# Row maxima of two neighbouring heads computed as a pair of short products in the two row halves of TensorE's array

## The reference, cut to what matters

```python
# layer 0
q, k = _apply_rotary(q, sin, cos), _apply_rotary(k, sin, cos)
scores = jnp.einsum('bhqd,bhkd->bhqk', q, k) / np.sqrt(HD)
scores = jnp.where(attn_mask[:, None, None, :], scores, -jnp.inf)
attn = jax.nn.softmax(scores, axis=-1)
out = jnp.einsum('bhqk,bhkd->bhqd', attn, v)
# layer 1
scores = jnp.einsum('bqgrh,bkgh->bgrqk', q, k) * (1.0 / np.sqrt(HD))
a = jax.nn.softmax(scores, axis=-1)
out = jnp.einsum('bgrqk,bkgh->bqgrh', a, v)
```

## Time and profile before

| | |
|---|---|
| time, median of 3 runs | 3960.23 us (3954.39 to 3964.08) |
| profiled execution, span of the core | 3966.3 us |
| PE busy | 3790.3 us, 96% of the span |
| DVE busy | 2467.7 us, 62% |
| ACT busy | 1601.7 us, 40% |
| POOL busy | 1603.3 us, 40% |
| mean granted TensorE clock | 0.976 of full speed |
| row-maximum products | 2048, of which 1760 in attention steps |

### The profile page before, as it was taken

One profiled execution on the slowest core, in us unless ns is written; L12 is line 12 of the kernel. 1 busy time (PEld: TensorE's weight loads), 2 busy tenths in 40 slices (PEclk: granted clock), 3 DMA queues, 4 the chain that ended last, 5 costly groups with the idle time before them and its releaser, 6 DMA issues.

```text
span 3966.3 us, 53519 instructions
## 1 busy us (share of the span) xinstructions
PE 3790.3 (96%) x20404; PEld 1507.3 (38%) x20404; DVE 2467.7 (62%) x3951; ACT 1601.7 (40%) x2807; POOL 1603.3 (40%) x907
## 2 busy tenths in 40 slices
PE   7988999999999999999999999999999999999999
PEld 4422444233443335432254323433244333533344
DVE  5687735766457655576654777367664776467752
ACT  1465313554125642155521663136521563126621
POOL 2466212673216632066510672136520672226611
PEclk8899999999999999999999999999999999999999
DMA  5233243212433123331233012311123112311122
GB/s 155 56 98 111 82 107 84 80 41 89 104 80 81 44 87 93 103 81 44 105 96 94 22 41 91 111 44 28 62 94 101 31 39 80 109 59 25 62 67 96
DMA packets 139021, 305.21 MB, mean 77 GB/s; under 512 B 19680, under 2 KB 59636, under 8 KB 137872
## 3 DMA queue, kind: packets, MB, share of 16 engines
q10 hardware_dynamic: 50944, 174.62, 13.6%
q1 hardware_dynamic: 87824, 127.17, 12.2%
HBM read 223.46 MB, written 36.66 MB: 66 GB/s over the span
## 4 chain that ended last, share of the span: by engine, by line
PE 83%; DVE 8%; POOL 3%; issue 3%; ACT 3%; DMA 1%; ACTq 0%; SPq 0%; POOLq 0%; DVEq 0%
PE ps L834 12%; PE ps L836 12%; PE ps L835 12%; PE ps L1014 11%; PE ps L935 9%; PE ps L997 8%; PE ps L871 7%; PE ps L1029 5%; DVE mcol L1517 3%; PE ps L888 3%; ACT probs L1194 2%; POOL sums L730 2%; DVE ring L1567 2%; PE ps L852 1%; DVE turn L1451 1%
## 5 line engine op out<-in xcount | busy, mean ns | idle before, releaser
L1517 DVE TENSOR_REDUCE mcol<-ps 128x1 f32<-128x512 f32 x2048 | 1288.5, 682 | 470.6 <-PE ps L935 470.2
L730 POOL TENSOR_TENSOR sums<-probs 128x1024 f32<-128x1024 f32 x448 | 1057.6, 2376 | 967.6 <-PE ps L1029 525.9
L1194 ACT ACTIVATE probs<-ps 128x512 f32<-128x512 f32 x2048 | 1098.2, 608 | 826.9 <-PE ps L997 592.8
L935 PE MATMUL ps<-ks,qs 97*128 97x512 f16 x2048 | 789.4, 389 | 61.3 <-DVE mcol L1517 43.6
L997 PE MATMUL ps<-qs,ks 98*128 98x512 f16 x2048 | 773.2, 387 | 72.3 <-ACT probs L1194 67.2
L1340 ACT ACTIVATE sums<-ps,cols 128x512 f32<-128x512 f32 x256 | 175.8, 687 | 1096.9 <-PE ps L836 1096.9
L1014 PE MATMUL ps<-probs,v_sb 128*32 128x512 f32 x4096 | 567.0, 628 | 0.0
L935 PEld LDWEIGHTS ps<-ks,qs 97*128 97x128 f16 x2048 | 201.2, 99 | 619.0 <-DVE mcol L1517 361.9
L834 PE MATMUL ps<-ring,probs 128*128 128x512 f16 x1024 | 388.0, 379 | 0.3 <-DVE probs L1612 0.3
L834 PE MATMUL ps<-aT,ring 128*128 128x512 f16 x1024 | 388.0, 379 | 0.0
L836 PE MATMUL ps<-aT,ring 128*128 128x512 f16 x1024 | 388.0, 379 | 0.0
(11 more groups left out here) (110 smaller groups left out, 3293.4 us busy)
## 6 DMA issues: line engine op xcount, KB each, us to landing
ring<-halves ACTq DMA_DIRECT2D x208, 512.0 KB, 3.4
qs<-hl SPq DMA_DIRECT2D x192, 128.0 KB, 4.0
ring<-halves SPq DMA_DIRECT2D x48, 512.0 KB, 6.3
ring<-in_weights ACTq DMA_DIRECT2D x39, 512.0 KB, 4.3
halves<-ring ACTq DMA_DIRECT2D x37, 512.0 KB, 2.9
ks<-hl SPq DMA_DIRECT2D x120, 128.0 KB, 4.3
dcopy<-inverses SPq DMA_DIRECT2D x56, 256.0 KB
probs<-in_x SPq DMA_DIRECT2D x8, 1024.0 KB, 8.3
```

Source lines behind the costliest of these rows:

```text
L730: pool.tensor_tensor(sums[:, m % SUM_SLOTS, :, :], prob(u - 2), prob(u), ALU.add).then_inc(sum_set[0].sem, 1)
L935: pe.matmul(bank, qs[0:K_MAX, hh, h, P * qt:P * qt + P], ks[0:K_MAX, key_set(i, hh), key_head(i, hh, h), 512 * half:512 * half + 512], sta ...
L1194: act.activation(prob(u)[:, e, :], ps[:, w % SCORE_BANKS, :], ACT.Exp).then_inc(exp_done.sem, 1)
L1517: dve.tensor_reduce(mcol[:, blk % 2, 4 * j + qt, half:half + 1], src, AX.X, ALU.max).then_inc(n_free[0], 1)
```

## The change

1. **Pairs.** In attention steps two maxima are made one after the other by the new `max_pair`: an even and an odd head of the same query tile and key half. The even head's product runs over rows 0 to 32 (layer 0) or 0 to 63 (layer 1), the odd head's over rows 64 to 96, so each needs one row half of the array. Only high halves are multiplied (in layer 1 the even head has a low term too). The waits for both PSUM banks stand ahead of the first product. The 288 maxima outside the attention steps stay single products over 97 rows.
2. **Order of a step.** Before: maximum and score in turn. Now: pair, score, score, score, pair, score (with a fill: its halves before the third score and before the second pair). `max_tile` orders the maxima so that neighbours are an even and an odd head, and `MAX_AT_K` has only even counts (twice six maxima in a step, elsewhere four).
3. **Stacks.** Odd heads have the planes in another order (`KEY_BASES`, `QUERY_BASES` and their layer-1 counterparts), the mask in row 96 for odd and in row 32 for even heads, and heads lie in slots by parity (`slot_of`). For that the projections' columns are permuted on the host, and `put_stack` issues 12 DMAs per stack in layer 0 (each half of the partitions and 4 heads) and 6 per query stack in layer 1; `put_rows` issues two, `key_rows` three in layer 0.

The 2048 scores, the reductions, exponentials, sums, values and the feed-forward part stay as they are.

Twice as many issues stand ahead of the row of maxima. The diff, cut to its core:

```diff
+KEY_BASES = (((0, 65), (33,)), ((32, 64), (0,)))
+QUERY_BASES = (((0, 33), (65,)), ((0, 64), (32,)))
+PAIR_ROWS = (slice(0, HD + 1), slice(2 * HD, 3 * HD + 1))
+MASK_ROW, MAX_ROW = (HD, 3 * HD), 3 * HD + 1
+PLAIN_PAIR_ROWS = (slice(0, 2 * HD), slice(2 * HD, 3 * HD + 1))
-MAX_AT_K = (0, 2, 5, 7, 9, 11, 14, 16, 18, 20, 23, 25, 27, 29, 32)
+MAX_AT_K = (0, 2, 4, 6, 10, 12, 14, 16, 20, 22, 24, 26, 28, 30, 32)
 def max_tile(k):
-    return k // 2 % 4, k // 8, k % 2
+    pair, odd = divmod(k, 2)
+    return 2 * (pair // 8) + odd, pair % 8 // 2, pair % 2
...
+def slot_of(g, j):
+    return 4 * (j % 2) + 2 * g + j // 2
...
             def put_stack(key):
...
                 if layer(i) == 0:
                     sp.wait_ge(st_lo, BUILDS[key] + 1)
-                    rows, heads, pieces = 16, slice(0, 8), [(0, 0), (0, 1), (1, 0), (1, 1)]
...
+                    for odd in range(2):
+                        half, slots = slice(64 * odd, 64 * odd + 64), slice(4 * odd, 4 * odd + 4)
+                        for low in range(2):
+                            for base in (KEY_BASES if kind == "k" else QUERY_BASES)[odd][low]:
+                                for x in range(2):
+                                    r = slice(base + ROT * x, base + ROT * x + ROT)
+                                    dst = ks[r, key_set(i, hh), slots, tok] if kind == "k" else qs[r, hh, slots, :]
+                                    sp.dma_start(dst, hl[half, 2 * low + x, :]).then_inc(done, 16)
...
             def put_rows(i, blk):
...
+                for odd in range(2):
+                    d = qs[MAX_ROW:MAX_ROW + 1, hh, 4 * odd + 2 * g:4 * odd + 2 * g + 2, :]
+                    dst = bass.AP(d.tensor, d.offset, [[d.ap[0][0], 1], [P, 8], [1, P]])
+                    sp.dma_start(dst, mT[8 * odd:8 * odd + 8, :]).then_inc(max_in.sem, 16)
...
+            def max_pair(two):
+
+                _, i, blk, k = two[0]
+                if k == 0:
+                    stacks_ready(i, blk)
+                banks = [bank_free(key) for key in two]
+                for bank, key in zip(banks, two):
+                    j, query, keys = max_operands(key)
+                    rows = (PAIR_ROWS if layer(i) == 0 else PLAIN_PAIR_ROWS)[j % 2]
+                    pe.matmul(bank, query[rows], keys[rows], start=True, stop=True).then_inc(n_full, 1)
...
                         maxima, fills = maxima_at(i, s), FILLS[i].get(s, [])
-                        some(maxima[0:1])
+                        pairs = [maxima[n:n + 2] for n in range(0, len(maxima), 2)]
+                        for two in pairs[0:1]:
+                            max_pair(two)
                         score(i, 4 * s)
-                        some(maxima[1:2])
                         score(i, 4 * s + 1)
                         for key in fills:
                             fill(key, 0, 6 if key[0] in "kqv" else 12)
-                        some(() if fills else maxima[2:3])
                         score(i, 4 * s + 2)
                         for key in fills:
                             if key[0] in "kqv":
                                 fill(key, 6, 12)
-                        some(maxima[2:3] if fills else maxima[3:4])
+                        for two in pairs[1:2]:
+                            max_pair(two)
                         score(i, 4 * s + 3)
-                        some(maxima[3:] if fills else maxima[4:])
+                        for two in pairs[2:]:
+                            max_pair(two)
```

More of the change, by code:

```diff
@@ new lines, in put_stack @@
+                    return
+                sp.wait_ge(*freed(key))
+                sp.wait_ge(st_hi, BUILDS[key] + 1)
+                for low in range(2):
+                    x = 2 * low + BUILDS[key] % 2
+                    if kind == "k":
+                        for base in SHARED_KEY_BASES[low]:
+                            sp.dma_start(ks[base:base + HD, key_set(i, hh), 0:4, tok], hl[:, x, :]).then_inc(done, 16)
+                        continue
+                    for odd in range(2):
+                        slots = slice(4 * odd + 2 * part, 4 * odd + 2 * part + 2)
+                        for base in PLAIN_QUERY_BASES[odd][low]:
+                            sp.dma_start(qs[base:base + HD, hh, slots, :], hl[64 * odd:64 * odd + 64, x, :]
+                                         ).then_inc(done, 16)
@@ L1710, in _ @@
             scales_0(1)
-            dve.wait_ge(s_rows, 64)
+            dve.wait_ge(s_rows, 96)
             for i in range(NB):
```

106 lines of the change are left out of this document (50 added, 56 removed).

## The result

| | before | after |
|---|---|---|
| median of four executions | 3959.94 us | 4043.01 us (4037.95 to 4051.57) |
| ratio to before, 95% interval | | 1.0213 (1.0198 to 1.0228) |
| profiled execution's span | 3966.3 us | 4041.5 us |
| mean granted TensorE clock | 0.976 | 0.964 |

The kernel became slower by 83 us. The forecast was 3974, with 4000 as the upper end: the way was right, the size was not.

A forecast was written before the change was run, and what follows sets the result against it. TensorE bounds, but barely: POOL's chain to the exponentials has 0.09 us of slack in 6.55. Layer 1 +1.3, layer 0 +6.1 and stacks +6 make +13.4 us on 3960.2: 3974 us, range 3945 to 4000.

The forecast's parts named there:

- The pair itself: Attention steps: 880 pairs replace 1760 products; the second runs beside the first, sparing 185 us of PE time.
- The changes of form: TensorE's switches into and out of row halves: 1384 more at 0.095 us each, 131 us come back.
- Clean pairs of steps: Attention's odd and even step together: 6.655 us instead of 6.55, 0.105 longer.
- the release of 0.06: Second pair of an odd step: starts 0.06 us after the reduction that frees its bank, at 1.17.
- The chain: From `totals` over POOL's sum to the exponentials: releases the even step's third score at 3.86, not 3.59.
- Steps with the transposed maxima: Attention steps with transposed maxima in front: one more change of form for the first pair, hidden in the wait: 0.
- Steps with a fill: Attention steps with a fill (2.6 us): waits are covered, PE gains 0.13 us each.
- Six maxima: Layer 0, two steps a batch: the third pair waits for a reduction, about 0.4 each, +0.8 us a batch.
- Stacks in layer 0: Twelve DMAs for step 6's second key stack delay the row of maxima: 1.4 us lost, +6 us in four batches (2 to 13).
- In layer 1: Stacks elsewhere than layer 0's step 6 have more time: no cost unless their cover falls under 4 us.
- rival 4: TensorE's clock falls more often, once in every fourth of 56 blocks with maxima: 25 us, 3999; chance 6%.

The follow-up runs named there:

- the ladder: Three kernels between before and changed: the layout alone 3975.9 us, `full_rows` 4024.1, both products of a pair in the same row half 4168.3.
- the table: Changed kernel with the kernel before's counts of maxima per step in layer 0's block 2 (five, four, five): 4034.2 us.
- the layout alone: Changed stacks and transfers, but single maxima over the full rows in the order and at the times of the kernel before: 3975.9 us, 1.0045.
- repeated scores: Changed kernel with scores ahead of long bank waits computed two to six times over: 4017.3 us; control, the kernel before with repeats in its waits: 3953.9 us.
- `full_rows`: Changed kernel with both products of a pair over all 97 rows, order, layout and transfers as changed: 4024.1 us, 1.0166.
- `one_wait`: Changed kernel in which a pair waits once, for the later of its two banks: 4026.4 us, 1.0173.
- two kernels of 3917 and 3919 us: Kernel before with POOL's additions in halves; changed layout with one pair a step and all remedies. With repeated scores: 3916.4 and 3919.0 us.
- the cut into halves: POOL's addition in two halves, each exponential waiting for its own: kernel before 3917.0 us (-44), changed kernel 4005.1 us.

## Why the forecast was wrong

The mechanism of the clean steps held. What failed is the step from them to the whole. The other steps, the queue in layer 1, the starts of batches and the clock were put at little or nothing, and they hold nearly all of the loss. Term by term:

- **The pair itself**: right. Two products take the time of one, and without the overlap a clean pair of steps takes 0.47 us more. The kernel takes 127 us more, up to 77 of them by the clock, where I had put 185 less what waits hide.
- **The changes of form**: right in price, 0.32 to and from a pair against 0.218. The sum of 131 us is not confirmed by the ladder's 145, since up to 125 of these may be the clock.
- **Clean pairs of steps**: right in sum, 6.67 against 6.655, but 2.90 + 3.77 instead of 2.79 + 3.87. I counted 67 of them, the trace before has 48; they cost 5.8 us where 7 were put. What failed here is the release of 0.06 taken for the second pair: two waits make it 0.146. The chain was right as the releaser of the third score (3.86 forecast; 2831.73 - 2827.88 = 3.85), yet a second bound stood within 0.02 us behind it, unread.
- **Steps with the transposed maxima**: put at 0; they take 3.98 instead of 3.81 us in 17 places of layer 1, 3 us.
- **Steps with a fill**: put at -0.13 each, "the waits are covered". Failed: the pair that follows a fill needs two banks before it and the score may start. In layer 1 the fill steps of blocks 1 and 3 and those behind them cost +0.25 and +0.13 a pair of steps; in layer 0's block 0 some are 0.25 to 0.5 longer and others shorter by as much, so that they give 0 at full clock instead of -0.9 a batch, and in the changed kernel their waits bring the clock down.
- **Six maxima**: put at 0.8 a batch; the table is worth 2.0 a batch in the mean, 9 us in the whole.
- **Stacks in layer 0**: right, 1.0 to 2.2 us a batch in the layout alone (forecast 1.4), with a landing of 2.6 us for 64 KB where 2.5 was put. **In layer 1** "at no cost" failed: the cover of the stack itself is long, but the inverses and the row of maxima behind it in the same queue had none. 1.0 to 2.0 us a batch.
- **Starts of batches**: missing. 12.6 us in layer 1, about 10 of them by the clock, and 6.7 us outside the attention, which were not traced further.
- **The clock** (rival 4, 6%, 25 us): mis-weighted. I argued that stretches with little work had kept it mostly at full. It was at half for 101 us more than before, and 26 us came back by repeated scores alone. Its estimate of 14 falls of 3.6 us, at 1.8 us each, was right in the price (1.67 measured) and half of the length: 13 stretches more, but 101 us in place of 50.

The sum worked out the clean pairs of steps with care and gave the other steps, in which DVE, a bank, a queue or ACT's table decides, small or no terms; these hold nearly all of the 83 us. The sign was right on a sum of small terms: the clean pairs (+7) and the stacks of layer 0 (+6) held, the fills (-8) did not, and most of what was measured lies in terms that were not there. To that extent the sign was luck. The single runs don't add up to it: 18 of the layout, 48 of the order and table (of which the table makes about 9 and the second wait about 15, as measured in the changed kernel), and 18 of the pairs' own account including the clock. The clock lies inside the last two, so the 20 us that repeated scores give back are not a further term. How the remainder of the order's share splits between fills, starts and transposed steps is read from the steps and was not run apart.

## What to carry to other kernels

Before two instructions are put together, list what each waits for: the pair and all behind it wait for the later of the two, and with three banks a group of two leaves one bank of slack. Price a reordering in the steps that are not clean (fills, block ends, first steps, queues with something behind) before the clean ones. When a chain bounds a loop, cutting the producer in halves with a wait for each is cheap and may be worth more than the engine that looks busiest: here 44 us for some ten lines.

## What the runs showed of the hardware

- Behind two waits on the same counter a TensorE product started 0.146 us after the event (changed kernel and `full_rows`), behind one after 0.058 (kernel before and `one_wait`).
- TensorE's clock fell to half in a stretch at 0.76 ahead of which the engine had been busy for 4.39 us of 5.94. 192 products that compute nothing new made a kernel 26 us faster; in two kernels of 3917 and 3919 us, with clocks of 0.983 and 0.979, they changed nothing.
- POOL's addition over 512 columns takes 1.27 us in the median where that over 1024 takes 2.36; the cut into halves costs 0.16 us of POOL's time an addition (1129.3 against 1057.6 us over 448).
- Twelve issues of 64 KB take SP 7.6 to 9.3 us, and each landed 2.6 us after its issue in the median, against 4.3 for 128 KB before and 3.0 for the 24 pieces of 128 KB that the changed kernel still has.
- Two products over 33 and 33, or 64 and 33, rows in different row halves started 0.003 to 0.006 us apart and took 0.39 us together; in the same half 0.60. Ahead of and behind such a pair stand 0.32 us start to start, where full-width products of 512 columns follow each other after 0.218.
